# Second attention heads: the relative-position bias is skewed by lines one element longer and written whole from SBUF

## The reference

```python
rel_idx = jnp.clip(pos[None, :] - pos[:, None], -32, 32) + 32
rel = rel_emb[rel_idx]
scores = jnp.einsum('bhqd,bhkd->bhqk', q, k)
scores = scores + jnp.einsum('bhqd,qkd->bhqk', q, rel)
scores = jnp.where(causal[None, None], scores, NEG_INF)
attn = jax.nn.softmax(scores, axis=-1)
ctx = jnp.einsum('bhqk,bhkd->bhqd', attn, v) + jnp.einsum('bhqk,qkd->bhqd', attn, rel)
```

## Time and profile before

| | us |
|---|---|
| median of 3 runs | 5097.98 |
| lowest, highest | 5095.38, 5112.85 |
| the profiled execution, its own time | 5106.48 |
| its span, first to last instruction | 5104.8 |
| PE busy | 4455.2 (87%) |
| DVE busy | 2996.9 (59%) |
| ACT busy | 2297.0 (45%) |
| POOL busy | 648.1 (13%) |

### The profile page before, as it was taken

How to read it: one execution, slowest core, us unless ns; L and a number is a source line. 1 busy time by engine, 2 the same in 40 slices (tenths; PEclk the granted TensorE clock), 3 DMA queues, 4 the chain that set the end, 5 groups by cost and what they waited for, 6 DMA issues and landing times. The chain is left out here.

```text
span 5104.8 us, 80050 instructions
## 1 busy us (share of the span) xinstructions
PE 4455.2 (87%) x25680; PEld 2625.2 (51%) x25680; DVE 2996.9 (59%) x5384; ACT 2297.0 (45%) x4375; POOL 648.1 (13%) x666
## 2 busy tenths in 40 slices
PE   7999859999999999889998965688978978889488
PEld 6888723333333333258886544345545545555355
DVE  6655668888888888456664355444444544444342
ACT  3222327777777777612222222334434434445222
POOL 2322100000000000013332024111111111111000
PEclk9999969999999999889999987778778878789699
DMA  2000311111111111039000026444444444341801
GB/s 77 0 0 1 138 50 42 42 39 41 37 37 42 42 38 33 11 113 296 0 0 18 0 86 183 112 93 93 103 95 95 105 94 96 97 98 44 133 26 33
DMA packets 316682, 343.08 MB, mean 67 GB/s; under 512 B 161280, under 2 KB 266760, under 8 KB 302600
## 3 DMA queue, kind: packets, MB, share of 16 engines
q1 hardware_dynamic: 299912, 296.20, 22.1%
q0 software_dynamic: 16384, 41.96, 2.9%
HBM read 239.26 MB, written 148.11 MB: 76 GB/s over the span
## 5 line engine op out<-in xcount | busy, mean ns | idle before, releaser
L1322 DVE TENSOR_REDUCE full_tops<-psum 128x1 f32<-128x1024 f32 x1024 | 1207.2, 1220 | 247.8 <-PE psum L1226 247.4
L1279 ACT ACTIVATE full_probs<-psum 128x512 f32<-128x512 f32 x2048 | 1067.2, 602 | 338.5 <-PE psum L1198 306.4
L1736 ACT ACTIVATE causal_probs<-psum 128x512 f32<-128x512 f32 (+3 forms) x1280 | 644.3, 533 | 761.2 <-PE psum L1622 389.4
L1784 DVE TENSOR_REDUCE causal_tops<-psum 128x1 f32<-128x1024 f32 (+7 forms) x704 | 587.4, 859 | 261.5 <-PE psum L1659 261.5
L1198 PE MATMUL psum<-full_q,full_k 49*128 49x512 f32 x2048 | 657.8, 482 | 49.5 <-ACT full_probs L1279 33.3
L1608 PE MATMUL psum<-causal_q,causal_k 49*128 49x512 f32 (+3 forms) x1280 | 465.3, 508 | 181.2 <-DMA causal_q<-causal_rows 171.0
L1198 PEld LDWEIGHTS psum<-full_q,full_k 49*128 49x128 f32 x2048 | 290.1, 189 | 640.4 <-ACT full_probs L1279 585.4
L1207 PE MATMUL psum<-full_probs,full_vh 128*32 128x512 f32 x4096 | 565.3, 625 | 0.7 <-ACT full_probs L1279 0.7
L1226 PE MATMUL psum<-full_k,full_q 48*128 48x512 f32 x2048 | 408.9, 463 | 64.7 <-DMA full_k<-qk_split 38.3
L1659 PE MATMUL psum<-causal_k,causal_q 48*128 48x512 f32 (+4 forms) x1152 | 375.2, 468 | 88.9 <-DMA causal_k<-rot_parts 46.9
L1638 PE MATMUL psum<-causal_probs,causal_vh 128*32 128x384 f32 (+3 forms) x3712 | 409.1, 501 | 1.2 <-ACT causal_probs L1736 1.2
(11 more groups left out here) (189 smaller groups left out, 6095.6 us busy)
## 6 DMA issues: line engine op xcount, KB each, us to landing
bias_tiles<-in_bias SPq DMA_DIRECT2D x4, 10240.0 KB, 86.5
causal_bias<-bias_tiles SPq DMA_DIRECT2D x32, 1280.0 KB, 27.7
band_scores<-xn POOLq DMA_DIRECT2D x192, 160.0 KB, 6.1
qk_split<-qkvf_parts SPq DMA_DIRECT2D x32, 512.0 KB, 3.4
full_q<-qk_split SPq DMA_DIRECT2D x64, 256.0 KB
full_k<-qk_split SPq DMA_DIRECT2D x64, 256.0 KB
rot_parts<-qkvc_parts SPq DMA_DIRECT2D x32, 512.0 KB, 3.1
causal_q<-rot_parts SPq DMA_DIRECT2D x64, 256.0 KB
```

The lines of the kernel that those rows point to most:

```text
L1279: nc.scalar.activation(pT[:, kt % 4, n * BLK:(n + 1) * BLK], k.psum[:, bank(q, u), :], ACT.Exp).then_inc(p_ready, 1)
L1322: nc.vector.reduce_max(mx[:, q % 2, u // 2, u % 2:u % 2 + 1], src, AX_X).then_inc(m_free, 1)
L1736: nc.scalar.activation(dst, k.psum[:, bank(q, u), 0:(hi - lo) * P], ACT.Exp).then_inc(p_ready, 1)
L1784: last = nc.vector.reduce_max(mx[:, r, t, entry:entry + 1], both[:, off:off + hi - lo], AX_X)
```

## The change

**Skew.** Bias rows of a head are now one line for each of the 128 queries of a tile: 16 tiles of 160 and one element more (BIAS_ROW = 2561), read back at 2560, so that row r is again shifted by r. The lines are put together in SBUF: `skew_rows` holds half a line (8 tiles) with the mask already in it, DVE copies 32 numbers for each tile into it (`spread`), and SP writes the half lines, 128x1280 and 128x1281, to `bias_tiles`. The relative scores come to SBUF in one transfer a head (`load_rel`, 128x512). The 4 filling transfers go, and a mask of 128x160 is loaded at the start of the stage. Because the buffer is one half line, DVE waits before each `spread` until the half before it has landed, and SP waits before each write for `spread`.

**Transfers.** Output and denominator of a column block are stored by one transfer (17 rows of `out_heads`' new form `causal_heads`), from one buffer `osb` in place of two. Band tiles: 4 pairs in place of 8, so DVE waits for the store of four steps before, in place of that of the head before.

**ACT.** `row` stands before the two exponentials of its step.

**Outputs.** `project_full_stage` loads the reciprocals broadcast, two transfers a block, and drops the PE product. `project_causal_stage` loads the numerator in two transfers of 8 heads in place of one.

```diff
@@ alloc_attention, fill_bias_tiles
-    k.BB = dram(k, "bias_tiles", (NH * KT * P * SKEW + SKEW,))
+    k.BB = dram(k, "bias_tiles", (NH * P * BIAS_ROW + 1,))
+    k.OD = dram(k, "causal_heads", (NH, VW, S))
-def fill_bias_tiles(k, sp):
...
@@ heads_causal_stage, SP
-                def skew(i):
-                    rows = k.BB[1:1 + NH * KT * P * SKEW].rearrange("(h t p c) -> h t p c", h=NH, t=KT, p=P)
-                    dst = rows[bass.ds(i, 1), :, :, 0:REL].rearrange("a t p j -> p (a t) j")
-                    src = k.TD[bass.ds(i, 1), :, :, :].rearrange("a p t j -> p (a t) j")
-                    sp.dma_start(dst, src).then_inc(skewed, 16)
+                def load_rel(i):
+                    if not isinstance(i, int) or i > 0:
+                        sp.wait_ge(spread_done, 2 * i)
+                    sp.dma_start(compact[:, :, :], k.TD[bass.ds(i, 1), :, :, :].rearrange("a p t j -> p (a t) j")).then_inc(rel_loaded, 16)
+                def skew(i, part):
+                    sp.wait_ge(spread_done, 2 * i + part + 1)
+                    lines = k.BB[1:1 + NH * P * BIAS_ROW].rearrange("(h p x) -> h p x", h=NH, p=P)
+                    dst = lines[bass.ds(i, 1), :, part * HALF_ROW:(part + 1) * HALF_ROW + part].rearrange("a p x -> (a p) x")
+                    sp.dma_start(dst, skew_rows[:, 0:HALF_ROW + part]).then_inc(skewed, 16)
+                def load_bias(i, q):
+                    heads = k.BB[0:NH * P * BIAS_ROW].rearrange("(h x) -> h x", h=NH)
+                    src = heads[bass.ds(i, 1), 0:P * KT * BAND].rearrange("a (r t c) -> (a r) t c", r=P, c=BAND)
+                    sp.dma_start(bt[:, q, :, :], src).then_inc(bt_loaded[q], 16)
...
-                        sp.dma_start(cols(k.ND[bass.ds(j * DH, DH), :]), blocks(osb[32 * b:32 * b + DH, r, :])).then_inc(o_stored[r], 16)
-                        sp.dma_start(cols(k.DD[bass.ds(j, 1), :]), blocks(osb[32 * b + DH:32 * b + VW, r, :])).then_inc(o_stored[r], 16)
+                        dst = k.OD[bass.ds(j, 1), :, :].rearrange("a r (m b n) -> (a r) m b n", b=QB, n=P)[:, :, b, :]
+                        src = osb[32 * b:32 * b + VW, :].rearrange("r (m n) -> r m n", n=P)
+                        sp.dma_start(dst, src).then_inc(o_stored, 16)
...
-                def body(i, q):
-                    load(i + 3, (q + 3) % 4)
-                    store(i - 1, (q + 1) % 2)
-                    row_load(i + 1, (q + 1) % 4)
+                def body(i, q, left):
+                    if left > 2:
+                        sp.wait_ge(skewed, 32 * (i + 4))
+                        sp.wait_ge(pv_done, (i + 3) * NSTEP + NSTEP)
+                        load(i + 3, (q + 3) % 4)
+                        load_bias(i + 3, (q + 3) % 4)
+                    if left > 3:
+                        skew(i + 4, 0)
+                    store(i - 1)
+                    if left > 3:
+                        skew(i + 4, 1)
+                    if left > 4:
+                        load_rel(i + 5)
+                    if left:
+                        row_load(i + 1, (q + 1) % 4)
@@ ACT
-                        exps(i, q, n, (3, 4))
                         if left and n == ROW_STEP + 1:
                             act.wait_ge(row_loaded[(q + 3) % 4], 32 * ((i + 3) // 4 + (q + 3) % 4 // 3))
                             row(i + 1, (q + 1) % 4)
+                        exps(i, q, n, (3, 4))
@@ DVE
-                        if not first:
-                            dve.wait_ge(band_stored[n], 16 * i)
+                        if n >= PAIRS:
+                            dve.wait_ge(band_stored[n - PAIRS], 16 * (i + 1))
+                        elif not first:
+                            dve.wait_ge(band_stored[n + PAIRS], 16 * i)
+                def spread(i, part):
+                    if part == 0:
+                        dve.wait_ge(rel_loaded, 16 * (i + 1))
+                    if not isinstance(i, int) or i + part > 0:
+                        dve.wait_ge(skewed, 16 * (2 * i + part))
+                    nc.vector.memset(skew_rows[:, HALF_ROW:HALF_ROW + 1], 0.0)
+                    wide = skew_rows[:, 0:HALF_ROW].rearrange("p (t c) -> p t c", c=BAND)
+                    tiles = slice(part * KT // 2, (part + 1) * KT // 2)
+                    nc.vector.tensor_copy(wide[:, :, 0:REL], compact[:, tiles, :]).then_inc(spread_done, 1)
...
+                        if at in (2, 8) and more:
+                            spread(i + 4, at // 8)
@@ project_full_stage
+                for c in range(C):
+                    every = src[c * HC:(c + 1) * HC, :].unsqueeze(1).to_broadcast([HC, DH, BLK])
+                    sp.dma_start(rd[:, half, c, :], every).then_inc(s_ld[half], 16)
...
-                    nc.tensor.matmul(k.psum[:, c, :], spread[0:HC, :], rd[0:HC, half, c, :],
-                                     start=True, stop=True).then_inc(rb_ready, 1)
```

More of the change, by code:

```diff
@@ L1409, in heads_causal_stage @@
         vh = sb("vh", [P, 2, KT, VP])
-        osb = sb("out", [P, 2, BLK])
+        osb = sb("out", [P, BLK])
         mx = sb("tops", [P, 2, KT, 3])
@@ L1447, in heads_causal_stage @@
         o_free = sem("o_free")
-        o_stored = [sem(f"o_stored{r}") for r in range(2)]
+        o_stored = sem("o_stored")
         mm_stored = [sem(f"mm_stored{r}") for r in range(2)]
@@ L1464, in band_tile @@
         def band_tile(n, i):
-            o = 2 * n + i
-            return head[:, o, :] if o < KT - 4 else tail[:, o - (KT - 4), :]
+            return bands[:, 2 * (n % PAIRS) + i, :]
         def band_pair(n):
-            o = 2 * n
-            return head[:, o:o + 2, :] if o < KT - 4 else tail[:, o - (KT - 4):o - (KT - 4) + 2, :]
+            return bands[:, 2 * (n % PAIRS):2 * (n % PAIRS) + 2, :]
         def segment(q, left):
@@ L1529, in _ @@
                 sp.wait_ge(ones, 4)
-                for q in range(3):
-                    load(q, q)
+                load(0, 0)
+                skew(0, 0)
+                skew(0, 1)
+                load_rel(1)
+                load(1, 1)
+                sp.wait_ge(skewed, 32)
+                sp.wait_ge(edge_set, 16)
+                load_bias(0, 0)
+                skew(1, 0)
+                skew(1, 1)
+                load_rel(2)
+                load(2, 2)
+                sp.wait_ge(skewed, 64)
@@ L1541, in _ @@
                 with sp.Fori(0, NH // 4 - 2) as it:
                     for q in (1, 2, 3, 4):
-                        body(it * 4 + q, q % 4)
-                for i in range(NH - 7, NH - 3):
-                    load(i + 3, (i + 3) % 4, i + 4 < NH)
-                    store(i - 1, (i - 1) % 2)
-                    row_load(i + 1, (i + 1) % 4)
-                for i in range(NH - 3, NH):
-                    store(i - 1, (i - 1) % 2)
-                    if i + 1 < NH:
-                        row_load(i + 1, (i + 1) % 4)
@@ L1552, in _ @@
-                store(NH - 1, (NH - 1) % 2)
+                        body(it * 4 + q, q % 4, 5)
+                for i in range(NH - 7, NH):
+                    body(i, i % 4, NH - 1 - i)
+                store(NH - 1)
+                sp.wait_ge(o_stored, 16 * QB * (NH + 1))
                 for r in range(2):
-                    sp.wait_ge(o_stored[r], 16 * (1 + 2 * QB * NH // 2))
                     sp.wait_ge(mm_stored[r], 16 * (1 + NH // 2))
@@ L1817, in _ @@
                         far(1, 1, p)
+                spread(3, 1)
                 def body(i, q, left):
-                    for ahead, h, p in segment(q, left):
+                    more = not isinstance(i, int) or i + 4 < NH
+                    for at, (ahead, h, p) in enumerate(segment(q, left)):
                         if p == 1 and ahead == 2:
@@ L1867, in project_full_stage @@
     bias = take(D)
-    spread = take(P)
     s_w, s_rec, s_rc = sem("weights"), sem("recip_dma"), sem("recip")
     s_ld = [sem(f"loaded{r}") for r in range(2)]
-    rb_ready = sem("rb_ready")
     o_ready = sem("o_ready")
```

110 lines of the change are left out of this document (62 added, 48 removed).

## The result

The changed kernel takes **5,411.27 us** (median of 4 runs, 5,398.4 to 5,437.74) against 5,097.97 before (5,095.38 to 5,112.85). The ratio is 1.0615, interval 1.0565 to 1.0664: 6% slower, where 4,750 was forecast. The sign was wrong.

A forecast was written before the change was run, and what follows sets the result against it. SP's closed ring of transfers, held by the skew, was taken to bound the causal heads, with PE's own work next. Terms -310 - 7 - 27 - 13 + 5 = -352 from 5,106.5 gave 4,754, forecast 4,750 us, range 4,670 to 4,900.

The forecast's parts named there:

- the landing of the half line: Causal heads: 640 KB behind 1,280 KB of bias lands in about 7 us, so DVE waits 1 to 2 us, PE none.
- 128-byte pieces from DRAM to DRAM are what was slow: Causal heads: the skew's 2,048 small pieces held SP for 20.85 us a head; a 5 KB write would take 0.75.
- The slower rival: Half line lands as late as the old skew, 29.2 us; slower beyond 22.9 a half; 380 us slower, 5,450; chance 0.05.
- the wait moves to the half lines: DVE's second spread waits for a later landing, PE 4 us late in 30 heads; about 4,960 us; chance 0.17.
- PE's own head: Causal heads: PE's work at full clock is 33.9 us a head and bounds once SP's ring is open.
- The waits for row and copy: Causal heads: PE's 146 us of waits for the row of maxima go whole, and 32 us for ACT's copy.
- Start of the stage: Causal stage before its first scores: 101.6 us falls to 74, a gain of 27, between 10 and 38.
- Loop edges: Causal loop, every four heads: 7 edges with a 1.3 us gap and a half-clock stretch remain, 46 us in all.
- ACT's copy: Causal heads: moved ahead of two exponentials, it ends before PE wants its bank; all 32 us gained, at least 20.
- First output: First attention's output: without the spreading product DVE bounds at 4.4 us a block; gain 13 us, between 4 and 18.
- Causal output: Causal output: one more transfer issued by SP in each of 8 blocks; 5 us slower, between 0 and 13.
- The rule on the number of DMA engines: Largest number up to 16 dividing both outermost sizes: 17-row store on one engine, hidden; numerator on eight, 13 us at most.

The follow-up runs named there:

- run 1: Changed kernel with rotated q and k laid head by head in DRAM, so their loads spread over all DMA engines: 5,011.22 us, ratio to before 0.9782.
- run 2: Kernel before the change with rotated q and k laid head by head in DRAM, nothing else: 4,850.94 us, ratio 0.9501.
- run 11: Changed kernel with only q laid head by head in DRAM, k left as it was: 5,178.33 us, ratio 1.0144.
- run 9: Changed kernel with each store of 17 lines split into 16 and 1, q and k as they were: 5,391.89 us, ratio 1.0581.
- run 5: Kernel before the change with q and k laid head by head and ACT's copy of the maxima ahead of the two exponentials: 4,768.82 us, ratio 0.9365.
- run 6: Changed kernel, q and k head by head, stores split 16 and 1, DVE's second spread at position 16, its write behind the row load: 4,781.9 us, 0.9369.
- run 7: As run 6, with stores to two tensors and both output stages as before the change: 4,762.9 us, ratio 0.936.
- run 8: As run 5, with the full attention's q and k also laid head by head: 4,772.07 us, ratio 0.9356.
- run 3: As run 1, with each store of 17 lines split into one of 16 and one of 1: 4,988.59 us, ratio 0.9757.

## Why the prediction was wrong

**The step that failed** is the landing of the half line: "640 KB behind 1,280 KB of bias is then about 7 us", from a store of 6.0 us alone in its queue. Measured: 24.2. The term counts nothing for the eight q and k loads ahead of both, 1.5 MB. The row that bounds it stood in the same group: bias itself lands after 27.7 us, and the half line is issued behind it. DVE's second `spread` waits for this landing, 17 us a head where 1 to 2 were forecast, and PE for DVE, 15 where none was.

**The reading behind it** is that SP "is held by this one transfer for 20.85 us", with "128-byte pieces from DRAM to DRAM are what was slow". The time at a queue's instruction, and to its landing, was taken as that instruction's own cost, so that it would go with the pieces. Two things were in it. The late landing is the backlog of the loads ahead (runs 1, 2 and 11). SP's hold was long only where this backlog met the skew (20.85 us) or the stores of 17 lines (24.89). With the loads spread it was 6.2 and 9.11; at a half line, with 5 KB pieces and the backlog in front of it, 0.36. So the change did take SP's hold at the skew away, and PE no longer waits for the row; but the late landing stayed, and the change puts DVE behind it. The stores were another miss of the sum, 24.89 us of SP in place of 4 x 0.75, but in run 9 this miss goes and the time moves by 0.3%, inside the intervals.

**The slower rival** had the right place (DVE's second spread), the right reason for the sum (the half lands as late as the old skew) and nearly the time, 5,450 against 5,411. I gave it 0.05, because I tied it to the shape of the write. Its deciding point, 22.9 us a half, is for two slow halves; only the first is slow, and the remaining 7 + 22 us of the ring do the rest. So its near hit in the time is partly luck. The rival at 0.17, *the wait moves to the half lines*, had the place too, and a cause that comes close ("bands and loads on the same engines"); it put 4 us on PE a head where 15 were measured.

**Right, once the loads are spread.** PE's own head: 33.9 forecast, 33.7 in runs 5 to 8. The waits for row and copy go whole. The row is issued 21 us into the head in run 7 (3756.32 after 3734.99), as forecast. The clock of the causal heads is 0.93 in run 7, 0.74 in the changed kernel. Runs 6 and 7, the change with its cause of delay removed, land at 4,782 and 4,763 beside the 4,750 forecast: the sum was that of another kernel. But so does run 5, with the old skew, at 4,769: beside the new order of q and k, the new skew is worth nothing measurable here.

**Small terms.** Start of the stage, from the end of the stage before to the first scores: -27 forecast, +16 measured (127.6 us, 3140.3 to 3267.86, against 111.8), with the first bias loaded only behind two half lines and the first heads' loads; in run 7 it is 90.6, -21. (The prediction's terms for this stretch add up to 73 us, not 74.) Loop edges: 6.6 us each forecast, 8.7 in run 7 (heads of 42.4 among 33.7). ACT's copy: of 32 us "all, at least 20" holds only with the row in time. First output: -13 forecast, +2 and -1 measured. PE waits 26.45 us for the first block in place of 20.59, and the later ones are little shorter than the 6.5 of before: at full clock 5.8 us (3.71 of projection and 2.06 of wait for DVE's product, one behind the other) where 4.4 was forecast from DVE's busy time alone, as if the two overlapped. Causal output: +5 forecast, 13 measured in this pair, at the end of the range. The rule on the number of DMA engines I applied to the new transfers alone and not to the loads that were there already; these decide.

## What to carry to other kernels

Time at a DMA instruction in a queue need not be that transfer's cost: look at the share of busy DMA engines while it stands, and if it is 2 of 16, look ahead of it for a load whose outermost size is 2. And it need not be what the others wait for: run 9 took 24.89 us of it away and the time stayed. Before a transfer is made cheaper, bound its successor's landing by the landing of what is queued just ahead of it. A buffer that is written twice a head through an in-order engine puts one landing on that engine; place the second write later than the landing, or the engine stands with all that is behind it.

## What the runs showed that was not expected

A transfer on all engines behind one on two waits for those two: 640 KB landed after 24.2 us, 19.2 with half of the load taken off, 13.7 with all, and after 3.3 with only small stores ahead (second half, run 3). Four stores of 17 lines, 136 KB in all, held SP for 24.89 us; 8 stores of 16 and 1 lines were issued within 10.2 us with q and k as they were, and held it for under 0.8 each with q and k spread. At an edge of the loop a head takes 42 us in place of 33.7, with three short gaps of PE in it:

```profile
3799.78 0.49 PE L1640 MATMUL psum<-causal_q,causal_k 49*128 49x512 f32 x1 [1.25 <-ACT causal_probs L1768]
...
3801.82 0.79 PE L1640 MATMUL psum<-causal_q,causal_k 49*128 49x512 f32 x1
...
3806.89 0.66 PE L1640 MATMUL psum<-causal_q,causal_k 49*128 49x512 f32 x3 [1.70 <-issue]
...
3809.26 0.58 PE L1640 MATMUL psum<-causal_q,causal_k 49*128 49x256 f32 x1 [0.76 <-ACT causal_probs L1768]
```
```profile
3800.00:3817.00 17.00, 14.54 (x75) 7.79 (x74) 7.51 (x24) 5.98 (x12) 2.21 (x4) 0.70 0.69 131
```

The first is PE's timeline of run 7 at an edge, the second the window around it: the granted clock is 0.70, part of the stretch at 1.2 GHz. The same product of 512 columns takes 0.49 us at 3799.78 and 0.79 at 3801.82, so the half clock is there before the gap of 1.70 us, behind one of 1.25.
